# One list of eight per row, second counts on VectorE, and a packed patch embedding in a fused attention and mixture-of-experts block

## The reference, cut to what matters

```python
tok = patches @ W + b                      # 36 patches of 768 values, to 256
h   = layernorm(concat([cls, tok]) + pos) * gamma + beta      # 37 image rows
h   = concat([h, txt], axis=1)             # 165 rows
q, k, v = split_heads(layernorm(h) @ W_qkv.T + b_qkv)         # 16 heads of 16
s   = q @ k.T * D ** -0.5                  # 165 scores per row, 16 * 165 = 2640 rows a batch
keep = the int(165 * 0.3) = 49 largest scores of each row     # the others become -inf
h   = h + (softmax(keep) @ v) @ W_out.T + b_out
h   = h + moe(layernorm(h))                # shared expert, and 8 of 64 routed experts, 128 slots each
```

## Time and profile before

| what | value |
|---|---|
| median of the three timed runs | 3364.08 us |
| profiled execution, its own time | 3362.61 us |
| its span, first to last instruction | 3360.9 us |
| busy: TensorE matmul, VectorE, ScalarE, GpSimd | 2740.0, 2809.3, 2785.1, 2167.3 us |
| mean granted TensorE clock | 0.934 |
| chain that ended last, share of the span | VectorE 38%, ScalarE 27%, TensorE 13%, issue 12%, DMA 4%, GpSimd 3% |

### The profile page before, as it was taken

How to read it: one execution, slowest core, us unless ns; L and a number is a source line. 1 busy time by engine, 2 the same in 40 slices (tenths; PEclk the granted TensorE clock), 3 DMA queues, 4 the chain that set the end, 5 groups by cost and what they waited for, 6 DMA issues and landing times.

```text
span 3360.9 us, 82985 instructions
## 1 busy us (share of the span) xinstructions
PE 2740.0 (82%) x22281; PEld 2098.7 (62%) x22281; DVE 2809.3 (84%) x11013; ACT 2785.1 (83%) x12673; POOL 2167.3 (64%) x3409
## 2 busy tenths in 40 slices
PE   4688888888888888888888888988888888647776
PEld 3466666666666666666666666666666666436665
DVE  1899999999999999999999999999999999822222
ACT  3999999999999999999999999999999999611111
POOL 3456767667676667767766676776676766444554
PEclk7899999999999998999999999999999999868888
DMA  1001100000000000000000000000000000016776
GB/s 51 11 14 20 20 21 21 21 21 20 14 20 20 21 21 21 21 15 19 20 20 21 21 21 21 18 17 20 20 21 21 21 20 17 11 38 158 174 176 139
DMA packets 181453, 116.34 MB, mean 35 GB/s; under 512 B 100208, under 2 KB 172484, under 8 KB 180964
## 3 DMA queue, kind: packets, MB, share of 16 engines
q1 hardware_dynamic: 146596, 91.60, 10.0%
q0 software_dynamic: 34368, 19.34, 3.9%
HBM read 66.51 MB, written 33.40 MB: 30 GB/s over the span
## 4 chain that ended last, share of the span: by engine, by line
DVE 38%; ACT 27%; PE 13%; issue 12%; DMA 4%; POOL 3%; DVEq 1%; SPq 1%; POOLq 0%; ACTq 0%
ACT JK L831 14%; DVE PR L1175 6%; DVE S L1028 5%; DVE ML L1070 5%; DVE MU L1047 4%; ACT E L819 4%; DVE XU L1037 4%; ACT SIDE L850 4%; DMA E<-x_rows,ids_t 2%; DMA out<-E,ids_t 2%; PE bank L1521 2%; DVE XL L1057 2%; PE bank L1676 1%; DVE RD L1180 1%; ACT PTT L861 1%
## 5 line engine op out<-in xcount | busy, mean ns | idle before, releaser
L831 ACT ACTIVATE JK<-S,thr 128x165 f32<-128x165 f32 x2688 | 1124.0, 442 | 3.4 <-POOL thr L562 1.7
L607 POOL DMA_INDIRECT slot_token<-TOKI,SLOT x512 | 541.3, 1057 | 202.8 <-issue 182.6
L850 ACT ACTIVATE SIDE<-S,t 128x165 f32<-128x165 f32 x1344 | 572.4, 447 | 9.4 <-POOL t L574 4.4
L831 ACT ACTIVATION_READ_ACCUMULATOR JK<-S,thr 128x1 f32 x2688 | 565.0, 210 | 0.0
L819 ACT ACTIVATE E<-bank,nb 128x165 f32<-128x165 f32 x1344 | 523.8, 418 | 14.6 <-DVE S L1028 14.4
L1175 DVE SCALAR_TENSOR_TENSOR PR<-S,TV,E 128x165 f32<-128x165 f32 x1344 | 434.1, 379 | 0.0
L1028 DVE TENSOR_SCALAR_CACHE_REDUCE S<-bank 128x165 f32<-128x165 f32 x1344 | 357.9, 314 | 12.5 <-PE bank L1504 10.5
L1047 DVE MAX8 MU<-XU 128x8 f32<-128x165 f32 x1344 | 349.2, 311 | 0.2 <-DVE XU L1037 0.2
L1070 DVE MAX8 ML<-XL 128x8 f32<-128x165 f32 x1344 | 339.7, 307 | 0.7 <-POOL XL L589 0.7
L1037 DVE SCALAR_TENSOR_TENSOR XU<-SIDE,S 128x495 f32<-128x495 f32 x448 | 317.0, 708 | 11.9 <-ACT SIDE L850 11.4
L589 POOL TENSOR_TENSOR XL<-SIDE,S 128x495 f32<-128x495 f32 x256 | 308.0, 1203 | 28.9 <-ACT SIDE L850 14.3
(11 more groups left out here) (196 smaller groups left out, 6981.8 us busy)
## 6 DMA issues: line engine op xcount, KB each, us to landing
S<-in_w_gate SPq DMA_DIRECT2D x64, 192.0 KB, 2.7
S<-in_w_up SPq DMA_DIRECT2D x64, 192.0 KB, 3.3
S<-in_w_down SPq DMA_DIRECT2D x64, 192.0 KB, 3.4
x_rows<-X SPq DMA_DIRECT2D x64, 160.0 KB
H<-in_txt SPq DMA_DIRECT2D x64, 128.0 KB, 5.9
QA<-QT SPq DMA_DIRECT2D x512, 10.3 KB
QB<-QT SPq DMA_DIRECT2D x512, 10.3 KB
out<-OT SPq DMA_DIRECT2D x64, 128.0 KB
```

Source lines behind the costliest of these rows:

```text
L607: pool.indirect_dma_start(slot_token, bass.IndirectOffsetOnAxis(SLOT[r % 2][:, 0, k:k + 1], 0), TOKI[r % 2][:, :], None, bounds_check=SLOT ...
L831: act.activation(JK[:, t % 4, :], S[r % 2][:, t, :], ACT.Sign, bias=(t0, t1)[n][:, t:t + 1], scale=-1.0, accum_out=(c0, c1)[n][:, t:t + 1] ...
L850: act.activation(SIDE[:, t % GROUP + GROUP * (g % 2), :], S[r % 2][:, t, :], ACT.Sign, bias=t2[r % 2][:, t:t + 1], scale=-1.0, accum_out=c ...
```

## The change

- **One list.** The side of t2 on which the 49th value lies is known from the third count: below if k is 49 or more, above otherwise. Two VectorE instructions for each of two sets of tiles turn `c2` into a sign per row (`side`, `side2`, giving `turn`). GpSimd computes `(S - t2) * turn` for each tile, 21 instructions of 128x165 with two per-row scalars (`apart`), in place of its four `under`. VectorE puts the wrong side out of play with one 128x495 instruction for each group (`one_side`, in place of `above` and of its three `under`), and takes one list of eight for each tile (`nearest`) instead of two. The picking works on one list with two ranks (`rank`, `candidates`, `threshold`), and the threshold is put together again (`threshold2`, `threshold3`). A row is now certain for k from 42 to 55, with the second test that the picked distance is at most half of t2's size (`exact`). ScalarE's third pass (`third_count`) writes its signs to a scratch tile and delivers only the count.
- **Second counts.** `AHEAD` is 9 instead of 12. ScalarE's second count covers tiles 0 to 8 only; tiles 9 to 20 are counted on VectorE (`second_count`, 12 instructions of 128x165 with an accumulated sum).
- **Packed embedding.** The patches of three batches are laid side by side (111 rows), and multiplied, normalized and scaled together, once in three iterations, into a tile `HP`. A DMA (`load_image`) then copies 37 rows of it into each batch's `H`. The statistics of `H` wait for it.
- **General path.** Its body is two nested loops over a tile and a round, with a wait after each instruction, in place of a body written out for three tiles at a time.
- **Order.** All four written orders are new. On GpSimd `front_center` stands near the end, between the two `refine2`, the indirect DMAs are grouped otherwise, and all seven `apart` stand before the first of them. On SyncE `load_text` stands behind both diagonals and the stores as before, `load_image` behind it and behind the patches of three batches, and `pack` is last instead of first.

The core of the diff:

```diff
-AHEAD = 4 * GROUP
+AHEAD = 3 * GROUP
-            def under(i, r, g):                                  # GpSimd, groups 0, 2, 4, 6
-                pool.tensor_tensor(XL[g % 3][:, :, :], SIDE[:, at:at + GROUP, :], S[r % 2][:, GROUP * g:GROUP * (g + 1), :],
-                                   ALU.mult).then_inc(s_xp, 1)
+            def apart(i, r, g):                                  # GpSimd, all groups
+                n = NG * i + g
+                pool.wait_ge(s_turn, TN * i + 2 * [g in v for v in SETS].index(True) + 2)
+                if n >= DEEP:
+                    pool.wait_ge(s_list, GROUP * (n - DEEP + 1))
+                gated()
+                for t in range(GROUP * g, GROUP * (g + 1)):
+                    last = pool.tensor_scalar(X[n % DEEP][:, t % GROUP, :], S[r % 2][:, t, :], t2[r % 2][:, t:t + 1], turn[:, t:t + 1],
+                                              ALU.subtract, ALU.mult)
+                last.then_inc(s_xp, 1)
...
+            def second_count(i, r, g):                           # VectorE, groups 3 to 6
+                    dve.tensor_scalar(JD[:, n % 3, :], S[r % 2][:, t, :], t1[:, t:t + 1], None, ALU.is_le, ALU.add,
+                                      accum_out=c1[:, t:t + 1]).then_inc(s_cd, 1)
+            def one_side(i, g):                                  # VectorE, all groups
+                dve.scalar_tensor_tensor(X[n % DEEP][:, :, :], X[n % DEEP][:, :, :], -BIG, X[n % DEEP][:, :, :], ALU.mult, ALU.min)\
+                    .then_inc(s_x, 1)
+            def nearest(i, g):
+                for t in range(GROUP * g, GROUP * (g + 1)):
+                    dve.max(LIST[:, 0, WIN * t:WIN * t + WIN], X[n % DEEP][:, t % GROUP, :]).then_inc(s_list, 1)
...
+            def load_image(b, r):                                # SyncE
+                n, at = (b + PACKED - 1) // PACKED, IMG * ((b + PACKED - 1) % PACKED)
+                ahead(sp, s_bd, BD * (b - RING) + 3, b - RING)
+                gated()
+                sp.wait_ge(s_gg, 4 * n + 4)
+                gated()
+                sp.dma_start(H[r][0:IMG, 1, :], HP[at:at + IMG, :]).then_inc(s_txt[r], 16)
...
-                    with dve.Fori(0, NG) as g:                   # general path
-                        for rnd in range(ROUNDS + 1):
...
+                    with dve.Fori(0, NT) as t:
+                        with dve.Fori(0, ROUNDS):
+                            dve.sem_clear(s_slow)
+                            dve.max(W8[:, :], W).then_inc(s_slow, 1)
+                            dve.wait_ge(s_slow, 1)
+                            dve.match_replace(W, W8[:, :], W, LOW).then_inc(s_slow, 1)
+                            dve.wait_ge(s_slow, 2)
```

More of the change, by code:

```diff
@@ L289, in parcels, with share, trio, of_trio @@
             return 16 * sum(m > 0 or at == PACKED - 1 for m in range(n % 2, n + 1, 2))
+        def share(i, groups, g):
+            return len(groups) * i + sum(k < g for k in groups)
+        TRIOS = (n_batch + PACKED - 1) // PACKED
+        def trio(m):
+            return m % PACKED == 0 and 0 <= m // PACKED < TRIOS
+        def of_trio(n):
+            return [b for b in range(PACKED * n - PACKED + 1, PACKED * n + 1) if b >= 0]
         def known(i):
@@ L686, in iteration @@
                     refine2(i, r, 0)
+                if has(i + 1):
+                    front_center(i + 1)
+                if has(i):
+                    refine2(i, r, 1)
+                if trio(i + 4):
+                    front_affine((i + 4) // PACKED)
                 if has(i - 2):
                     back_scale(i - 2)
-                if has(i):
-                    refine2(i, r, 1)
+                if True:
+                    packed(i, 2)
             def iteration(i, r):
+                if i == -1:
+                    front_scale(0)
+                    front_affine(0)
                 if has(i - 4):
@@ L906, in iteration @@
                 if has(i):
-                    exps(i, r, 2)
-                if has(i - 1):
-                    side(i - 1, (r - 1) % RING, 3)
+                    count(i, r, 0, range(0, AHEAD))
                 if has(i - 2):
@@ L1305, in iteration @@
                 if has(i - 1):
-                    above(i - 1, (r - 1) % RING, 1)
-                    lowers(i - 1, 0)
-                if has(i + 1):
-                    front_embed2(i + 1)
-                if has(i - 1):
-                    under(i - 1, (r - 1) % RING, 1)
-                    above(i - 1, (r - 1) % RING, 2)
-                    uppers(i - 1, 1)
+                    one_side(i - 1, 0)
                 if has(i):
@@ L1316, in iteration @@
                 if has(i + 1):
-                    front_norm(i + 1, (r + 1) % RING)
+                    front_norm_aggr(i + 1)
+                if has(i - 1):
+                    one_side(i - 1, 1)
+                    nearest(i - 1, 0)
+                    one_side(i - 1, 2)
+                if has(i + 1):
+                    front_norm2(i + 1, (r + 1) % RING)
                 if has(i - 3):
                     back_glu(i - 3)
-                if has(i):
-                    take(i, r, 4)
-                if has(i - 1):
-                    uppers(i - 1, 2)
+                if trio(i + 4):
+                    front_embed((i + 4) // PACKED)
                 if has(i - 3):
@@ L1346, in iteration @@
                 if has(i - 1):
-                    above(i - 1, (r - 1) % RING, 5)
+                    places(i - 1)
+                    one_side(i - 1, 5)
+                    places2(i - 1)
+                if has(i):
+                    take(i, r, 5)
                 if has(i - 3):
                     back_top3(i - 3)
-                if has(i):
-                    take(i, r, 5)
-                    take(i, r, 6)
+                if has(i - 1):
+                    one_side(i - 1, 6)
+                    nearest(i - 1, 4)
                 if has(i - 3):
                     back_weights(i - 3)
+                if has(i):
+                    take(i, r, 6)
                 if has(i - 1):
-                    lowers(i - 1, 3)
+                    nearest(i - 1, 5)
                 if has(i - 3):
```

741 lines of the change are left out of this document (386 added, 355 removed).

## The result

The changed kernel takes 3760.35 us (median of four runs, 3752.66 to 3766.23) against 3365.26 us before: ratio 1.118, 95% interval 1.112 to 1.124. It is slower by 395 us. The forecast was 3250 us with a range from 3105 to 3430. The profiled execution took 3766.23 us.

The account below looks back on a forecast made before the run. VectorE and ScalarE bounded the kernel before; GpSimd was to bound it after: 42.1 + 0.7 of waits = 42.8 us a batch against 44.65, -117 us over 63 batches, +5 at the start, 3250 us, range 3105 to 3430.

Parts of the forecast that it names:

- the price of `apart`: GpSimd's 21 `apart` a batch, 0.46 us each by line 536, +10.9 us in all, ends 9.8 and 11.9.
- The bound: GpSimd takes over as the bound at 42.1 us a batch (41.0 to 43.0), 2.3 us above VectorE.
- VectorE and ScalarE: Busy times a batch after the change: VectorE falls by 4.2 to 38.1 us, ScalarE by 4.9 to 37.6.
- `second_count`: Twelve counts on VectorE at 0.25 us each, +3.0 us a batch, bounds 2.8 to 3.7.
- The pause: VectorE's uncovered flag load and jump over the general path, 1.65 us a batch, kept; at most 0.4 could go.
- The rest of GpSimd's sum: GpSimd's other terms a batch: 38.65 us occupied, less 5.1 for `under`, 2.0 for embedding, 0.4 for pauses.
- the pauses before indirect DMAs: GpSimd's pauses, 4.5 us a batch before; `packed` 0 and 1 priced at 0.41 instead of 0.60, saving 0.4.
- Cheaper GpSimd: Rival: `apart` at 0.407 us and shorter DMA pauses give GpSimd about 40.5 us a batch; 3103 us; chance 13%.
- Late image copy: Rival: waits on the embedding's DMA into `H` add 2 us a batch; no gain, 3330 to 3397 us; 17%.
- VectorE holds `apart` back: Rival: VectorE's two-input SBUF instructions stretch GpSimd's `apart`; 0.65 us each gives 3500 us, 0.758 gives 3645; chance 11%.
- General path: Rival: one row outside the one list runs the body, 84 to 238 us, taken as 190; 3440 us; chance 8%.
- The first rival: Cheaper GpSimd: `apart` at 0.407 us, VectorE's 40.45 us with waits then sets the batch; 3103 us; chance 13%.

Follow-up runs that it names:

- e1: Changed kernel with `apart` adding a threshold negated by two small VectorE instructions, in place of subtracting; 3138.43 us, ratio 0.932.
- e5: e1 with the flag written just before the last mask instead of five masks before the general path; 3189.13 us, ratio 0.949.
- e3: Changed kernel with `apart` as an addition with one row scalar and the constant 1.0, lists wrong, flag held at 0; 3080.67 us, ratio 0.914.
- e8: e1 with the twelve second counts back on ScalarE, at the end of its order; 3400.80 us, ratio 1.011.
- e6: e1 with the general path's body, never entered, written out four times without the inner loop; 3169.22 us, ratio 0.943.
- e7: Kernel before the change with `sure_rows` ten masks earlier and the flag two masks earlier; 3371.78 us, ratio 1.003.
- e11: Kernel before the change with two GpSimd lines (536 by a row scalar, 524 on two tensors) subtracting instead of adding; 3400.16 us in one run.
- e9: e1 with GpSimd's second-half thresholds ahead of the indirect writes before them; 3513.70 us, ratio 1.036; rerun on another chip, 3177.02 us.

## Why the prediction was wrong, step by step

- **The step that failed** is the price of `apart`: "the nearest row is line 536, the same operation and shape with one row scalar instead of two". The shape was the same, the operation wasn't: line 536 adds, `apart` subtracts. The profile's row names both TENSOR_SCALAR; only the code tells them apart. Measured: 0.928 us, of which the subtraction is 0.44 and the second row scalar 0.08. I had allowed nothing for either. The 0.46 came near the median of the addition with two, 0.477, by luck, and was short even of its mean, 0.585. "Ends 9.8 and 11.9" for 21 held no bound for a difference between the forms; the measured 20.7 lies far outside. With it the forecast's own sum is 42.1 - 10.9 + 20.7 + 0.7 = 52.6 us a batch, against 50.9 measured.
- **The bound was right**: GpSimd, with 1.5 us of waits for others (forecast "about 1"), VectorE waiting before `one_side` and `second_count`. Because GpSimd was the bound, the error went into the time. But the forecast had GpSimd 2.3 us above VectorE at the low price already, and that isn't so: in e1 GpSimd is occupied for 41.24 - (38.6 + 24.2) / 36.4 = 39.5 us, by the forecast's own way of counting, and VectorE for 38.9 and a pause of 0.26, so neither bounds the batch alone.
- **VectorE and ScalarE** came within 1.5 us: 39.6 and 38.1 busy against 38.1 and 37.6. Mis-sized there is `second_count`: 0.381 us with a neighbour's overlap of 0.07 is a step of 0.31, not 0.25, so 3.7 us for twelve. It was the upper bound I had named.
- **The pause** of 1.65 us a batch, which I kept, is down to 0.27. I overlooked in the written order that the flag comes five masks ahead of the general path, so that load and jump are covered (e5: 0.8 us of it), and the load is short (0.30 for 1.08). The pause lies on VectorE, which wasn't the bound, and so the error cost nothing in the changed kernel. It counts in e1.
- **The rest of GpSimd's sum** was 1.7 us too dear (52.6 against 50.9). Part of it is the pauses before indirect DMAs, now (73.5 + 18.3) / 29.5 = 3.1 us for 4.1.
- **The rivals.** *Cheaper GpSimd*: no; e3, whose `apart` has this rival's price (0.403 us) at the cost of wrong lists, took 3081 us, near its 3103. *Late image copy*: refuted, 7.3 us of waits for it in the whole run. *VectorE holds `apart` back*: its figures (0.65 us: 3500; 0.758: 3645) came nearest the measured time, but its mechanism isn't the one, by the minimum of 0.910. A part of it exists: in e1 nine `apart` take 5.41 us, 0.60 each, over a median of 0.477, and those that overlap `one_side` are the stretched ones (0.786 against 0.488). *General path*: no instruction of its body has a row, so its prices of 0.46 and 0.5 us are untested.
- **Two slips** in the working change nothing above. The first rival takes VectorE's 40.45 us though it has GpSimd at 40.5 before the waits; 41.2 with them would have given 3150 us and not 3103. And the average of 84 and 238 us is 161, so the upper end by its own words is 3411, or 3440 with the 190 of the rival, not 3430.
- **What was the change worth without the failed step?** e1 is the change with about the price that I had assumed, and gives 3138 us where I said 3250: without the subtraction the direction is right and the size 112 us short. Its window:

```profile
1000.00:2500.00 1500.00, 1302.20 (x11484) 1024.62 (x11484) 1413.55 (x6235) 1375.52 (x6222) 1227.26 (x2339) 0.98 0.09 22
```

VectorE is 94% busy again, ScalarE 92%, GpSimd 82% besides its pauses before the indirect DMAs, at (2732.2 - 134.3) / 63 = 41.24 us a batch.

## What to carry to other kernels

Price an instruction by a row with the same *operations and operand kinds*, read in the code, and not by a row of the same name and shape; where none exists, let the range hold a factor of two before you let an engine with no room carry it 1344 times. On GpSimd, negate the scalar and add. And judge work that lies in a loop between engines by the loop's length, not by anyone's busy time: twelve counts moved were worth 262 us in e8 (the jobs differ; against e6 of the same job 232), where busy time had promised 80 to 130. And before you keep a pause in a forecast, read in the new order what will cover it.

## What the runs showed of the hardware

- GpSimd's tensor_scalar with a subtraction takes 0.843 to 0.928 us for 165 elements a row, with an addition 0.403 to 0.477; its tensor_tensor costs the same with either (0.727 and 0.726 us for 256). VectorE's subtraction: 0.356.
- A GpSimd `apart` that overlaps a VectorE instruction with two inputs in SBUF (`one_side`) takes 0.786 us in the mean in e1, one that overlaps no such instruction 0.488; 1.111 and 0.936 in the changed kernel.
- The load of one value into a VectorE register takes 0.30 us in the changed kernels, and 0.3 to 2.1 in the kernel before, e7 and e11. Long ones start mostly 2 to 4 us behind SyncE's second x_rows store and end 3.5 to 4.5 us behind it. What holds them is open.
- From a taken branch's end to its target VectorE takes 0.14 to 0.16 us in 54 of 64 batches over the short body (e1), and 0.45 to 0.50 in 55 of 64, 1.9 to 3.1 in the others, over one written out four times (e6).
- TensorE can stand still in a straight stretch of short matmuls with no wait that the profile shows: 437 us before the weight loads of one line of e9, in one job on one chip. On three other chips no kernel shows it as strongly, while the kernel before differed by under 1% between all of them. Cause open.
